# A new order for the last stretch of a three-stage language tower: four layers, then two output pairs, and part of the last sum on VectorE

## What is computed

```python
xn = layernorm(x) * gamma + beta
logits = xn @ Wr + br                       # 8 experts
top_vals, top_idx = top_k(logits, 2)
w = softmax(top_vals)                       # w_full: the two weights, 0 elsewhere
y = 0
for e in range(8):
    h = gelu(xn @ W1[e] + b1[e])            # 64 -> 128
    y = y + (h @ W2[e] + b2[e]) * w_full[..., e, None]   # 128 -> 64
out = x + y
```

## Time and profile before

| what | value |
|---|---|
| median of 3 runs | 684.34 us (684.22 to 685.77) |
| the profiled execution's own time | 684.15 us |
| its span | 682.4 us |
| TensorE (PE) busy | 93% of the span |
| VectorE (DVE), ScalarE (ACT), GpSimd (POOL) busy | 78%, 66%, 50% |
| `drain` on TensorE | about 649 to 679.4 us of the span |

### The profile page before, as it was taken

One profiled execution on the slowest core, in us unless ns is written; L12 is line 12 of the kernel. 1 busy time (PEld: TensorE's weight loads), 2 busy tenths in 40 slices (PEclk: granted clock), 3 DMA queues, 4 the chain that ended last, 5 costly groups with the idle time before them and its releaser, 6 DMA issues.

```text
span 682.4 us, 19223 instructions
## 1 busy us (share of the span) xinstructions
PE 631.3 (93%) x5077; PEld 432.5 (63%) x5077; DVE 530.5 (78%) x1953; ACT 448.7 (66%) x1385; POOL 343.1 (50%) x440
## 2 busy tenths in 40 slices
PE   2582997999999999999999999999999999999998
PEld 0471774456667667666667777776776666667635
DVE  4998888976777788888888778887777888887664
ACT  6990998014566667777666677667776667776673
POOL 2000000944356666665566666666556666655553
PEclk9999999889999999999999999999999999999999
DMA  6200000001444444444454455544444444444464
GB/s 205 114 0 0 2 0 1 7 33 62 95 95 103 102 101 101 101 102 101 104 117 110 114 113 111 116 121 101 101 101 101 101 101 101 102 101 103 87 118 94
DMA packets 61471, 60.42 MB, mean 89 GB/s; under 512 B 21972, under 2 KB 56900, under 8 KB 60932
## 3 DMA queue, kind: packets, MB, share of 16 engines
q1 hardware_dynamic: 59012, 59.35, 36.6%
q10 hardware_dynamic: 2240, 0.73, 0.4%
q0 software_dynamic: 192, 0.01, 0.0%
HBM read 55.19 MB, written 4.89 MB: 88 GB/s over the span
## 4 chain that ended last, share of the span: by engine, by line
PE 84%; DVE 9%; ACT 2%; issue 2%; DMA 1%; SPq 0%; POOL 0%; ACTq 0%; DVEq 0%; POOLq 0%
PE bank L1571 15%; PE bank L1441 13%; PE bank L1559 8%; PE bank L1560 7%; PE bank L1502 5%; PE bank L1522 4%; PE bank L1463 4%; PE bank L1476 3%; PE bank L1452 2%; PE bank L1480 2%; PE bank L1336 2%; PE bank L1298 2%; PE bank L1430 2%; PE bank L1347 2%; PE bank L1327 2%
## 5 line engine op out<-in xcount | busy, mean ns | idle before, releaser
L644 ACT ACTIVATE skill_rows<-bank,b1T,w_scale 128x512 f32<-128x512 f32 x256 | 196.6, 777 | 19.9 <-PE bank L1560 14.0
L478 POOL TENSOR_TENSOR feat_parts<-skill_rows 128x512 f32<-128x512 f32 x62 | 78.9, 1273 | 90.3 <-DVE feat_parts L1043 85.8
L1571 PE MATMUL bank<-skill_rows,w_sb 128*64 128x256 f32 x928 | 116.4, 382 | 0.0
L1441 PE MATMUL bank<-feat_parts 128*128 128x256 f32 (+1 forms) x512 | 102.2, 333 | 1.4 <-DVE feat_parts L1043 0.9
L1571 PEld LDWEIGHTS bank<-skill_rows,w_sb 128*64 128x64 f32 x928 | 63.1, 137 | 37.4 <-issue 11.0
L1441 PEld LDWEIGHTS bank<-feat_parts 128*128 128x128 f32 x512 | 79.6, 191 | 7.3 <-DVE feat_parts L1043 1.6
L1043 DVE TENSOR_TENSOR_SCAN feat_parts<-same,feat_parts 128x512 f32<-128x512 f32 x62 | 72.2, 1205 | 0.0
L1049 DVE TENSOR_TENSOR feat_parts<-bank,mask_sb 128x128 f32<-128x128 f32 x128 | 36.3, 284 | 38.6 <-PE bank L1441 37.7
L668 ACT ACTIVATE bank<-bank 128x64 f32<-128x64 f32 x128 | 26.6, 220 | 50.9 <-PE bank L1531 50.9
L1136 DVE SCALAR_TENSOR_TENSOR skill_rows<-bank,b2T,skill_rows 128x256 f32<-128x256 f32 x120 | 49.7, 475 | 3.6 <-PE bank L1571 2.5
L1065 DVE SCALAR_TENSOR_TENSOR feat_parts<-bank,feat_parts 128x256 f32<-128x256 f32 x128 | 45.0, 412 | 7.7 <-PE bank L1502 7.7
(11 more groups left out here) (278 smaller groups left out, 1526.1 us busy)
## 6 DMA issues: line engine op xcount, KB each, us to landing
skill_rows<-w_d SPq DMA_DIRECT2D x32, 512.0 KB, 6.6
same<-factor_d SPq DMA_DIRECT2D x31, 512.0 KB, 5.5
feat_parts<-w_d SPq DMA_DIRECT2D x30, 512.0 KB, 6.1
skill_rows<-skill_row_d SPq DMA_DIRECT2D x4, 1024.0 KB, 7.9
out<-o_sb SPq DMA_DIRECT2D x28, 128.0 KB, 5.1
feat_parts<-w_d SPq DMA_DIRECT2D x4, 256.0 KB, 4.8
w_sb<-in_L_ffn_W ACTq DMA_DIRECT2D x2, 256.0 KB
w_d<-wT SPq DMA_DIRECT2D x32, 16.0 KB, 1.4
```

The source lines that it names most:

```text
L478: pool.tensor_tensor(half[:, n, :], tm[:, 2 * n, :], tm[:, 2 * n + 1, :], ALU.add).then_inc(po_half, 1)
L644: act.activation(hid[:, e, :], banks[e % len(banks)][:, :], ACT.Gelu, bias=b1T[:, e:e + 1], scale=w1_scale[:, e:e + 1]).then_inc(ac_gelu, 1)
L1441: last = pe.matmul(n_bank[sc % 2][:, 0:SPAN[sc]], xs[:, k, sc * P:(sc + 1) * P], xs[:, k, sc * P:sc * P + SPAN[sc]], start=(k == 0), stop= ...
L1571: last = pe.matmul(z_bank[q % 2][n * D:(n + 1) * D, at:at + S // 2], w2_sb[:, e, :], hid[:, e, n * (S // 2):(n + 1) * (S // 2)], start=Tru ...
```

## The change

TensorE's order between `drain_out(a, 2)` and the end is new. `centred_T(c)` stands in front of b's layers; b's layers run four and four, b's first two output pairs follow each other, and c's four output pairs stand together behind all its layers. `drain_fold` of inputs 28 and 29 moves behind c's first four layers and behind `drain_out(b, 3)`, and `drain_fold(b)` behind c's last output pair. On ScalarE the weights' copy of c stands behind b's eighth GELU, not its sixth. On VectorE two instructions are new: `last_pairs` adds c's weighed pairs 0 and 1 (512 columns), and `last_halves` adds the two halves of that (256 columns). TensorE folds this one sum in place of experts 0 to 3 of c, after experts 4 and 5 and before 6 and 7. Some of VectorE's finishes move too.

```diff
@@ scalar drain
-                for e in range(4, 6):
+                for e in range(4, E):
                     gelu(b, e, drain_h)
                 weights_T(c)
-                for e in range(6, E):
-                    gelu(b, e, drain_h)
@@ vector
+            def last_pairs():
+
+                dve.wait_ge(dv_last, 4)
+                dve.tensor_tensor(last_two[:, 0], last_tm[:, 0], last_tm[:, 1], ALU.add).then_inc(dv_two, 1)
+
+            def last_halves():
+
+                dve.wait_ge(dv_two, 1)
+                dve.tensor_tensor(last_one[:, 0], last_two[:, 0, 0:S // 2], last_two[:, 0, S // 2:S], ALU.add)\
+                   .then_inc(dv_one, 1)
@@ vector drain
                 drain_weigh(a, 3)
+                drain_weigh(b, 0)
+                drain_weigh(b, 1)
                 drain_finish(B - 4)
-                for q in range(NP):
-                    drain_weigh(b, q)
+                drain_weigh(b, 2)
+                drain_weigh(b, 3)
                 drain_finish(a)
-                for q in range(NP - 1):
-                    drain_weigh(c, q)
+                drain_weigh(c, 0)
+                drain_weigh(c, 1)
+                last_pairs()
+                drain_weigh(c, 2)
+                last_halves()
+                drain_weigh(c, 3)
                 drain_finish(b)
-                drain_weigh(c, NP - 1)
                 last_finish()
@@ tensor
+            def last_fold(rows, first=False, last=False):
+
+                for c in range(2):
+                    done = pe.matmul(h_bank[c][:, 0:P], rows[:, c * P:(c + 1) * P], ident_f[:], start=first, stop=last)
+                if last:
+                    done.then_inc(pe_fold, 1)
+
+            def last_expert(q, e):
+
                 pe.wait_ge(dv_last, 2 * q + e + 1)
+                last_fold(last_tm[:, q, e * (S // 2):(e + 1) * (S // 2)], first=(2 * q + e == 4), last=(2 * q + e == E - 1))
@@ tensor drain
                 drain_out(a, 2)
-                drain_hidden(b, 0)
                 centred_T(c)
-                drain_hidden(b, 1)
+                for e in range(4):
+                    drain_hidden(b, e)
                 logits(c, 1)
                 drain_out(a, 3)
-                drain_hidden(b, 2)
-                drain_hidden(b, 3)
+                for e in range(4, E):
+                    drain_hidden(b, e)
                 drain_out(b, 0)
-                drain_hidden(b, 4)
-                drain_hidden(b, 5)
                 drain_out(b, 1)
                 weights_T(c)
-                drain_hidden(b, 6)
-                drain_hidden(b, 7)
-                drain_fold(B - 4)
                 for e in range(4):
                     drain_hidden(c, e)
+                drain_fold(B - 4)
                 drain_out(b, 2)
-                drain_out(b, 3)
                 drain_hidden(c, 4)
                 drain_hidden(c, 5)
-                drain_out(c, 0)
+                drain_out(b, 3)
                 drain_fold(a)
                 drain_hidden(c, 6)
                 drain_hidden(c, 7)
-                drain_out(c, 1)
-                drain_out(c, 2)
+                for q in range(NP):
+                    drain_out(c, q)
+                drain_fold(b)
+                pe.wait_ge(ac_gelu, E * B)
                 for e in range(2):
-                    last_fold(0, e)
-                drain_fold(b)
-                drain_out(c, 3)
-                for q in range(1, NP):
-                    for e in range(2):
-                        last_fold(q, e)
+                    last_expert(2, e)
+                pe.wait_ge(dv_one, 1)
+                last_fold(last_one[:, 0])
+                for e in range(2):
+                    last_expert(3, e)
```

More of the change, by code:

```diff
@@ L196, in program @@
         last_tm = over(parts_flat, 2 * S, NP, S)
+        last_two, last_one = over(parts_flat, 9 * S + CAUSAL, 1, S), over(parts_flat, 10 * S + CAUSAL, 1, S // 2)
         idle_rows = pm[:, 0:16]
@@ L244, in program @@
         dv_relu, dv_last = sem("dv_relu"), sem("dv_last")
+        dv_two, dv_one = sem("dv_two"), sem("dv_one")
         dv_gap, dv_w, dv_tm, dv_out, dv_lg = sem("dv_gap"), sem("dv_w"), sem("dv_tm"), sem("dv_out"), sem("dv_lg")
@@ L1625, in drain_fold @@
                 fold(b, 4)
-            def last_fold(q, e):
-                if q + e == 0:
-                    pe.wait_ge(ac_gelu, E * B - 2)
-                pe.wait_ge(dv_last, 2 * q + e + 1)
[L1632 to L1637, removed]
+            def last_fold(rows, first=False, last=False):
[4 more added lines that the diff above has]
+            def last_expert(q, e):
+                pe.wait_ge(dv_last, 2 * q + e + 1)
+                last_fold(last_tm[:, q, e * (S // 2):(e + 1) * (S // 2)], first=(2 * q + e == 4), last=(2 * q + e == E - 1))
             def drain():
```

## The result

The changed kernel takes 682.42 us (median of 15 runs, 681.95 to 683.95) against 684.33 us before (15 runs): ratio 0.9975, 95% interval 0.9967 to 0.9983. The medians differ by 1.9 us or 0.28%; the ratio with its interval is an estimate of its own and says 0.25%. The forecast was 682.3. The whole interval lies under 1, so the kernel is faster, but it reaches to both sides of the 0.3% (2.05 us) on which the prediction's chances turn, so it can't be said on which side of that the kernel lies.

The account below looks back on a forecast made before the run. TensorE was taken to bound the end: savings of 1.45 + 0.35 + 0.25 + 0.16 = 2.2 us, 2.0 with the pair add held, took the 684.34 us median to a forecast 682.3, range 681.6 to 683.8.

Parts of the forecast that it names:

- TensorE's queue sets the end: From 657.43 us to the last fold, only instructions taken from TensorE's queue count, until a wait comes up.
- The transposes in front: c's transposes before b's layers: 0.25 us from covering ScalarE's copy, 0.16 from logits costing 0.10 instead of 0.26.
- The order: Fewer output groups on TensorE behind a's pair 2, five instead of seven: entering and leaving costs 1.30, not 1.65 us.
- the stations: Predicted finishing times on TensorE, step by step: logits 659.56, c's four output pairs ending at 674.30, fold b 674.68.
- Three folds fewer: At TensorE's end, four of c's experts become one folded sum: 3 x 0.48 = 1.45 us less.
- The pair add is held: VectorE's 512-column add waits for GpSimd's last add for b until 673.90, costing TensorE 0.3 us.
- rival 2: VectorE bounds the end, the pair add taking 1.03 us plus a hold: gain 1.6, 682.7 us; chance 0.12.
- The router's bias add is held: VectorE's `logit_bias` for c waits for GpSimd's add, ending 1.2 us later; 1 us of slack, price nothing.
- rival 3: c's weights land late by DMA; past 674.45 all adds in full, 1 us more makes 683.0; chance 0.16.
- Rival 1: Nothing holds VectorE's pair add: 2.2 to 2.3 us gained, 682.1; chance 0.60 together with the forecast.
- Rival 4: Gain taken back elsewhere, by fold b waiting for GpSimd or the last store behind b's: about 683.3; chance 0.12.

Follow-up runs that it names:

- eight_folds: Changed kernel without VectorE's two adds, TensorE folding all eight experts of c: stretch (end of `drain_out(a, 2)` to last fold) 20.87 us; timed 683.35 us, ratio 0.9985.
- sum_only: Kernel before with VectorE's two adds and five last folds, in the old order of layers and outputs: stretch 20.56 us; timed 683.23 us, ratio 0.9987.
- transposes_back: Changed kernel with c's transposes behind b's first layer and its logits behind the second: stretch 20.52 us; timed 683.13 us, ratio 0.9985.
- hold_read: c2_first plus an unused 512-column add on GpSimd, started when expert 4 of c is weighed: stretch 20.82 us, pair add 1.59 us.
- hold_write: c2_first plus an unused 1024-column memset on GpSimd, started when expert 4 of c is weighed: stretch 19.9 us, pair add 0.68 us.
- late_weights: Changed kernel with one more 256 KB read between c's early and late weights: stretch 21.03 us, 0.94 more than the changed kernel.
- c2_first: Changed kernel with VectorE weighing c's pair 2 ahead of the pair add: stretch 20.03 us; timed 682.57 us, ratio 0.9970.

## Why the prediction was right

- **TensorE's queue sets the end.** Right: eight_folds, sum_only and transposes_back each moved the stretch by what they took off TensorE or put back, but for the waits named.
- **The transposes in front, 0.25 + 0.16.** Right: 0.43 in transposes_back.
- **The order, 0.35.** Right for the layers and outputs: they end at 16.93 against 16.87. Together with the transposes it is 0.76 in the sum; eight_folds shows 1.08. The 0.3 more lies in the last folds, as follows. (The terms add up to 2.21 and the stations, without the hold, to 2.29; the 0.08 between them is rounding, and the forecast's 2.0 is the stations' 2.29 less the wait of 0.3.)
- **Three folds fewer, 3 x 0.48 = 1.45.** This term was mis-sized. I had divided 2.89 by six, and had put an entry of 0.12 only on the first two. The two rows together already gave (2.89 - 1.09) / 4 = 0.45 a fold. The eight folds behind the fold of b cost 0.449 each with no entry; six at that price leave 0.20 of 2.89 for the entry, and two leave 0.19 of 1.09; the new order saves both entries and pays 0.15 for the fold of b, 0.24 in all, where the prediction had the one of 0.12 against that 0.15. In the changed kernel the five folds cost 2.48, so they pay an entry of 0.24, behind a wait. What the sum takes off TensorE in the new order is 3.59 - 2.48 = 1.11 us, less the wait of 0.31 (0.68 from the last output pair to the first last fold, against 0.37 for the fold alone): 0.80 in place of 1.45 - 0.3.
- **The pair add is held, 0.3 lost.** Right in mechanism and size: 0.93 us, its end 0.55 behind GpSimd's, 0.68 from the end of the last output pair to the first last fold as in the sum. hold_read and hold_write show the cause. The add itself is at 0.68, so rival 2 did not come up.
- **The router's bias add is held and costs nothing.** Right: 1.04 us, the merge 1.0 us ahead of the transpose.
- **The late weights have 0.35 of slack (rival 3).** Right in kind: late_weights adds 0.94 us by it, and what is late adds in full. The slack was larger, about 0.8, since the weights landed 16.1 us into the stretch and not 16.7.
- **Rival 1, no hold.** It did not come up. What it would have gained, no run shows: c2_first takes the hold away by another order, in which the weigh of pair 2 would start 16.1 us into the stretch and not at 17.0, and so meets the late weights at once. In the changed kernel's own order the add without the hold would end 0.25 us earlier (0.93 - 0.68), and pair 2 would still come behind its weights; so the 0.2 to 0.3 more of the prediction stays an estimate.
- **Rival 4 did not come up.** The fold of b waited for nothing: GpSimd was done at 674.80, TensorE came to it at 675.21. From the last fold to the end of the span it is 3.0 us before and 2.9 after, so the stores took nothing back.

The sum was 2.0, the stretch shows 1.86: 0.06 more in the layers and outputs and 0.07 more in the five folds (2.48 against 2.41). That the forecast median is off by only 0.1 us is partly luck. The sum on VectorE was worth 0.80 in the new order and not 1.15, and the order 1.08 and not 0.76; the two errors have one source, the entries into the last folds that were divided into the price of a fold, and cancel.

## What to carry to other kernels

Work that is moved from the bounding engine to a less loaded one brings its own waits: ask what the second engine's queue does at that moment, and whether a third engine reads SBUF then. When two savings meet in one stretch, price them together, since they may wait for the same thing. When a wait is removed by a new order, look at what that order asks for sooner: here the weights from DMA. Divide a row by its count only after taking off the cost of entering the group, which two rows of different counts give.

## What the runs showed of the hardware

- A VectorE add with two SBUF operands that meets a running GpSimd add of SBUF operands ends 0.55 us behind it (512 columns) whatever its own start: it took 0.92 or 0.93 us in the changed kernel, late_weights and transposes_back, and 1.59 in hold_read. A GpSimd memset of 0.96 us doesn't hold it (0.68 us). The Trainium skill says this of the shared port (SBUF — State Buffer, "Who interferes with whom"): only a GpSimd instruction that reads SBUF contends with a VectorE instruction of two SBUF inputs. These runs agree on both halves.
- The 512-column add of two contiguous f32 operands takes 0.68 us on VectorE, that of 256 columns 0.42.
- One execution can differ from the next by more than a change is worth: the same code reached the start of the stretch (the end of `drain_out(a, 2)`) at 657.43 to 658.54 us in the profiles whose start is given here, with TensorE's granted clock from 0.90 to 0.83 between 100 and 150 us in the two kernels compared above. The clock there is not all of it: c2_first had 0.93 in these 50 us and came to that point only at 658.18. Why the clock rises later in some executions stays open.
